# Rounding of the image rows moved into the attention's first seven items

## The reference, cut to what matters

```python
vis = bitnet_linear(dinov2_features, W_d2v, b_d2v)      # 4 x 1601 image rows
image_embeds = bitnet_linear(vis, W_img, b_img)
fused = bitnet_linear(text_embeddings, W_txt, b_txt)    # 4 x 512 text rows
for Wa, ba in ((W_att0, b_att0), (W_att1, b_att1)):
    kv = bitnet_linear(image_embeds, Wa, ba)            # rounds image_embeds first
    k = concatenate([kv, kv])
    attn = softmax(fused @ k.T / 16)
    fused = fused + 0.1 * attn @ k
```

## Time and profile before

| what | value |
|---|---|
| median of 3 runs | 2553.82 us (2547.07 to 2555.61) |
| the profiled execution: its own time | 2555.11 us |
| span of its profile | 2553.8 us |
| mean granted TensorE clock | 0.903 |
| busy in the span: PE, DVE, ACT, POOL | 2060.4, 1710.5, 1198.9, 857.0 us |
| rounding of all 16 chunks on DVE | 314.67 to 332.14 us |
| first exponential of the attention | 341.88 us |
| first and last product scaled (L1449) | 355.51 and 601.0 us |

### The profile page before, as it was taken

One profiled execution on the slowest core, in us unless ns is written; L12 is line 12 of the kernel. 1 busy time (PEld: TensorE's weight loads), 2 busy tenths in 40 slices (PEclk: granted clock), 3 DMA queues, 4 the chain that ended last, 5 costly groups with the idle time before them and its releaser, 6 DMA issues. The chain is left out here.

```text
span 2553.8 us, 45980 instructions
## 1 busy us (share of the span) xinstructions
PE 2060.4 (81%) x17234; PEld 1349.0 (53%) x17337; DVE 1710.5 (67%) x3403; ACT 1198.9 (47%) x2235; POOL 857.0 (34%) x673
## 2 busy tenths in 40 slices
PE   5886579986589994777798989877887887787877
PEld 3555157873479983443244444444555544555544
DVE  5875977768956665666677777737777435777553
ACT  2232866646333332322255555546665434666442
POOL 1110034331056661012276768553221223221141
PEclk8986789999689997888899999988999998998999
DMA  4211034451351113332322322011000001000000
GB/s 147 56 48 44 1 92 131 141 167 50 132 219 51 49 46 113 89 84 84 85 76 73 90 77 69 24 51 61 1 1 1 25 1 52 1 1 1 34 9 25
DMA packets 107467, 159.65 MB, mean 63 GB/s; under 512 B 26064, under 2 KB 85236, under 8 KB 104180
## 3 DMA queue, kind: packets, MB, share of 16 engines
q1 hardware_dynamic: 102836, 144.64, 18.5%
q0 software_dynamic: 4416, 12.06, 1.6%
HBM read 109.42 MB, written 47.19 MB: 61 GB/s over the span
## 5 line engine op out<-in xcount | busy, mean ns | idle before, releaser
L3016 DVE TENSOR_REDUCE xa_max<-psum 128x1 f32<-128x1024 f32 (+1 forms) x256 | 246.3, 987 | 94.0 <-PE psum L2927 89.3
L3099 ACT ACTIVATE xa_work<-psum 128x1024 f32<-128x1024 f32 (+1 forms) x208 | 212.9, 1025 | 185.8 <-PE psum L2950 174.4
L3156 POOL TENSOR_TENSOR xa_ctx_f<-xa_ctx_f,xa_work 128x1024 f32<-128x1024 f32 x96 | 226.9, 2364 | 44.2 <-ACT xa_work L3099 36.8
L3333 PE MATMUL psum<-xa_c_parts,x_hl_f 128*128 128x512 bf16 x536 | 138.7, 403 | 62.0 <-ACT qk_raw_l L3543 20.6
L2927 PE MATMUL psum<-xa_key_rows,xa_query_rows 96*128 96x512 bf16 (+1 forms) x512 | 131.9, 350 | 29.1 <-DVE xa_max L3016 15.4
L2967 PE MATMUL psum<-xa_work,xa_values 128*32 128x128 f32 (+1 forms) x3328 | 141.1, 287 | 0.0
L1087 POOL TENSOR_TENSOR text_q<-text_q 128x512 bf16<-128x512 f32 x64 | 81.1, 1270 | 177.0 <-ACT text_q L1505 176.6
L2950 PE MATMUL psum<-xa_query_rows,xa_key_rows 98*128 98x512 bf16 (+1 forms) x416 | 130.4, 396 | 11.2 <-DVE xa_max L3016 11.2
L3580 ACT ACTIVATE w_p_l<-psum,w_max_l 128x256 f32<-128x256 f32 (+1 forms) x256 | 110.6, 459 | 56.4 <-DVE w_max_l L3482 56.4
L1837 PE MATMUL psum<-moe_rows,moe_w 128*128 128x256 bf16 x1104 | 130.3, 276 | 4.9 <-issue 4.9
L2096 ACT CAST x_ch<-moe_raw 128x512 bf16<-128x512 f32 x92 | 56.9, 618 | 158.9 <-DVE moe_raw L2011 149.7
(11 more groups left out here) (484 smaller groups left out, 5015.4 us busy)
## 6 DMA issues: line engine op xcount, KB each, us to landing
text_q<-in_moe_w SPq DMA_DIRECT2D x64, 256.0 KB, 3.5
experts<-text_q SPq DMA_DIRECT2D x64, 256.0 KB, 2.8
moe_w<-experts SPq DMA_DIRECT2D x16, 1024.0 KB, 8.9
xa_key_rows<-cross_keys SPq DMA_DIRECT2D x48, 200.1 KB, 3.4
ctx_chunk<-in_ctxT SPq DMA_DIRECT2D x24, 300.0 KB, 3.0
cross_keys<-xa_k_hl SPq DMA_DIRECT2D x6, 800.5 KB, 3.7
moe_w<-pairs_out SPq DMA_DIRECT2D x8, 512.0 KB, 7.5
xa_ctx_f<-in_ctxT SPq DMA_DIRECT2D x4, 800.5 KB, 5.1
```

The lines of the kernel that those rows point to most:

```text
L3016: v.tensor_reduce(t["maxes"][n % 2][:, qt * HU + a, part:part + 1], u.wide[:, 0:c1 - c0], AX.X, ALU.max).then_inc(*u.free)
L3099: act.activation(t["exps"][k % EXPS][0:rows], u.wide[0:rows].rearrange("p (m q) -> p m q", q=T), ACT.Exp, scale=1.0 / float(np.sqrt(np.flo ...
L3156: g.tensor_tensor(total, other, exps, ALU.add).then_inc(*s.added.up())
L3333: ins = pe.matmul(b.ap, x[:, i, h, w * P:(w + 1) * P], t["wqkv"][:, j, h, cols], start=(h, n) == (0, 0), stop=(h, n) == (1, 2))
```

## The change

Only chunks 0 to 4 are rounded before the attention. The other eleven are steps of the plan that VectorE alone obeys, at the head of items 0 to 6: two each in items 0 to 3, one each in items 4 to 6. Round 1's side steps move: none in item 0; "asked" and three keys in item 1; the last key and a value in item 2; three values in item 3. TensorE's wait before a key product now asks for the rounding of the whole batch and no longer of the one chunk.

```diff
     for i in range(2 * ITEMS):
         more = i + 1 < 2 * ITEMS
+        plan += [("round", c) for c in ROUNDED_AT.get(i, [])]
         side = [step for step in sides.get(i, []) if step[0] != "asked"]
         plan += [("turn", i, 0), ("turn", i, 1), ("copy", i, 0), ("copy", i, 1)]
...
+ROUNDED_FIRST = 5
+ROUNDED_AT = {0: [5, 6], 1: [7, 8], 2: [9, 10], 3: [11, 12], 4: [13], 5: [14], 6: [15]}
...
-        for place, (a, e) in enumerate(((0, 3), (3, 5), (5, 7), (7, 9))):
+        for place, (a, e) in enumerate(((0, 0), (0, 4), (4, 6), (6, 9)) if r == 1 else ((0, 3), (3, 5), (5, 7), (7, 9))):
             sides[TPB * (r - 1) + place] = steps[a:e]
...
+def round_dve(m, s, t, n, c):
+    c0, c1 = CHUNKS[c]
+    for h in range(HALVES):
+        quantize_dve(m, s, t, n, t["q8"][:, h, c0:c1], t["wide"][:, h, c0:c1], P, h and 16 * (n - 1) + c + 1)
...
-    rounded(2)
+    rounded(2, range(ROUNDED_FIRST))
...
-            pe.wait_ge(*s.quantized(32 + 2 * c + 2))
+            pe.wait_ge(*s.quantized(32 + 8 * (c // 4) + 8))
...
+        if kind == "round":
+            round_dve(m, s, t, 2, step[1])
```

More of the change, by code:

```diff
@@ L1214, in scale, with rounded @@
         v.wait_ge(*s.scaled.now())
[L1216 to L1219, removed]
+    def rounded(n, chunks):
+        for c in chunks:
+            round_dve(m, s, t, n, c)
     scale(3, TEXT_MAX, TEXT_MAX + B, (("txt", 4),))
@@ L1224, in bitnet_inputs_dve @@
     scale(1, 0, 2 * len(CHUNKS), (("img", 1),))
-    rounded(1)
+    rounded(1, range(len(CHUNKS)))
     for c in range(len(CHUNKS)):
```

## The result

The changed kernel is slower: 2560.61 us against 2551.66 us in the same comparison (14 runs each), a ratio of 1.004 with a 95% interval of 1.0026 to 1.0053. That is 9 us where 10.9 were forecast (2565 us, from the 2553.8 of the first three runs). The change is clear of zero; the interval reaches down to 0.26%, so this comparison alone does not clear the 0.3% that counts as no change. A second comparison gave 1.0047 (1.0032 to 1.0061), which does.

The account below looks back on a forecast made before the run. VectorE was taken to bound the end of the inputs, by only 4.39 us, and TensorE items 1 to 6. The terms -4.4 + 0 + 15.3 = +10.9 us on 2553.8 gave 2564.7, say 2565 us; range 2553 to 2572.

Parts of the forecast that it names:

- Part 1: End of the inputs: eleven chunks (11.3 us) leave VectorE's run, but only 4.4 us are gained, as ScalarE ends at 328.41.
- Part 2: Item 0: two chunks (2.06 us) are covered by VectorE's idle time and the leaving key parts; 0, bounds 0 and 1.7 us.
- Part 3: Items 1 to 6 without any contention: chunks between scaling and copy lengthen items 1, 2, 3 and 5, +4.0 us in sum.
- Part 4: Items 1 to 6: roundings at the head wait for GpSimd's SBUF work, 1.0 to 2.3 us an item; growth +15.3 us in all.
- The roundings never wait: Rival for the item heads: GpSimd's instructions shift away or yield, so no waits; 2553.4 us, not slower; chance 0.22.
- VectorE's idle time takes it all: Rival: idle time absorbs the roundings and TensorE gets the full clock for scores or item 0's product; 2547.8 us; chance 0.08.
- The clock falls in the stretched items: Rival: TensorE idles in items like 2 and 3, products slow by 1.6 us, two to four times; 2568 to 2571 us; chance 0.15.

Follow-up runs that it names:

- e7: The changed kernel run again with no edit, for a second profile: items 1 to 6 took 63.3 us; 1.0047 of the kernel before in the second comparison.
- e1: Kernel before with only round 1's side steps moved an item later, all sixteen chunks still rounded ahead: 1.0003 (0.9994 to 1.0012) of before.
- e2: Changed kernel with GpSimd's expert step and its addition to x_tok cut to 8 columns each: 0.9987 (0.9977 to 0.9997) of the kernel before.
- e4: Changed kernel with eleven chunks rounded ahead, the other five at the head of items 0 to 4: 1.0014 (1.0005 to 1.0023) of the kernel before.
- e5: Changed kernel with the same eleven chunks at the end of items 0 to 7, ahead of the product: 0.998 (0.9971 to 0.999) of the kernel before.
- e6: Changed kernel with eleven chunks ahead, the other five at the end of items 0 to 3: 0.9981 (0.9971 to 0.9992) of the kernel before.

## Why the prediction was right

**Part 1** (-4.4) held: ScalarE's query sum came 4.5 us earlier, and VectorE stood idle for the other 7.1.

**Part 2** (0) failed by 3.1 us (2.3 in e7), in the direction of a gain. I had written that removing the key products gains nothing, since the product waits for the copy behind the load. Only its last ten matmuls do. What held up the others was, by the order of the outputs, the PSUM bank, the one four outputs back (the trace names no releaser here): with two key products between, that is the bank of the third transposition, which ScalarE reads behind the load; without them it is the first one's, read long before. The rows of e1 and of before fit this: the product starts at 350.70 in before, right behind ScalarE's copy of the third transposition (350.02 to 350.60), and at 346.84 in e1. No run changes the bank alone. That the gain comes from the side steps, e1 shows by itself; a part of it is that the last ten matmuls ran at the full clock there and in the changed kernel (1.38 us), as they did not in e2, e4, e5, e6 and e7 (2.0 to 2.5 us), and it is smaller by that much where they don't. VectorE's two chunks in item 0 were covered, as said, although they waited 1.9 us for GpSimd (2.57 us for a pair of roundings at 341.25), and so TensorE's second eight matmuls of the product waited 0.90 us for VectorE's copy while ScalarE still waited for its load.

**Part 3** (+4.0) held, by e2: 50.8 us for the six items, against the 51.0 that its lengths sum to.

**Part 4** held in kind. The waits in items 1 to 6, from a chunk's first instruction to the copy less 1.03 us a chunk, were 0.95, 2.2, 0.8, 1.9, 2.2 and 2.2 us, together 10.3; I had 11.7. The mis-sized one is item 3, where I took 2.1: item 2's product was so slow that GpSimd's first step and `x_tok` were over before the roundings began. That is the clock, which I had kept as a rival of its own: it cost 2.5 us in item 2 (5.59 against 3.1). The two are one event, as the slow product is also what spared item 3 its wait, so the clock's net price is about 1.2 us, and the sum of 15.3 stands against 16.6 measured. One sum of part 4 is added wrong: with waits of 1.0 us in all six items its own terms give 1.9 + 2.6 + 2.3 + 0.8 + 1.2 + 0.8 = 9.6 us, not 8.6, and the time for that case 2559 us, not 2558. Nothing else hangs on it.

**What was luck.** The terms missed by 3.1 us of gain in item 0 and by 1.3 us of loss in the items, and these point opposite ways: so 9.1 us came out where 10.9 were forecast. The kind of the loss, waits for GpSimd at the head of the items, was right; that the sum came within 2 us is partly the two errors offsetting each other.

The page "SBUF — State Buffer" of the Trainium skill, section "Who interferes with whom", says that a VectorE instruction in a two-port mode and one of GpSimd exclude each other; no run here shows the mode of the roundings. The trace agrees for VectorE: with GpSimd's work cut down (e2) the roundings are back to 0.46 and 0.65 us. For GpSimd no row here shows a block of a whole rounding: its rows grow by 0.12 us where a rounding takes some 0.33. And the rows show an order: by their times, the two engines take turns, instruction by instruction, and VectorE waits for one instruction of GpSimd each time.

**The rivals.** "The roundings never wait" fell by the rows of item 4 and by e2. "VectorE's idle time takes it all" fell with the item lengths. "The clock falls in the stretched items" came true for item 2, and in the second profile for items 2 and 5, but its price is lower than I had it, since a late product moves GpSimd's work out of the way.

## What to carry to other kernels

Work moved off a serial run gains only up to the engine that comes next behind it: look for its last instruction before counting. Where it is moved to, idle time of the engine isn't enough. It has to be idle time at that place in its order, with nothing that another engine's buffers wait for behind it, and with no GpSimd work on SBUF beside it; eleven chunks at the head of the items (nine of them in items 1 to 6) stretched these from 47.0 to 63.5 us, eleven at their end (seven in items 1 to 6) to 51.3. A side step that leaves can give more than its duration: two key products of 0.84 us together left item 0, and its scaling came 2.9 us earlier, probably because the product then waits for another PSUM bank.

## What was not expected of the hardware

- GpSimd and VectorE share the wait unevenly. Where both want SBUF, VectorE's roundings grow from 0.42 to 1.25 us and from 0.65 to 2.02 for a pair, while GpSimd's rows grow from 1.16 to 1.28 us and from 0.73 to 0.85.
- A product at the low clock costs once and pays some of it back, since the next item's roundings then come after GpSimd's work and not beside it: in e7, 12.1 us in item 5 (10.5 in the first profile) and then 8.9 in item 6 (10.9).
